# A graph network's attention head: segment scans on scores in PSUM, without the copy to SBUF

## What is computed

```python
h = (x @ W_i).reshape(n, H, C)                      # H = 4 heads, C = 32
e = es[src] + ed[dst]                               # a score for each edge and head
e = where(e > 0, e, 0.2 * e)
m = segment_max(e, dst)
p = exp(e - m[dst])
alpha = p / segment_sum(p, dst)[dst]
out = segment_sum(alpha[:, :, None] * h[src], dst)
```

## Time and profile before

| | us |
|---|---|
| device time, median of 3 (lowest to highest) | 9148.24 (9145.92 to 9149.09) |
| span of the profiled execution, first to last instruction | 9145.7 |
| VectorE busy | 5425.3 (59%) |
| GpSimd busy | 5269.3 (58%) |
| TensorE matmul busy | 5627.4 (62%) |
| ScalarE busy | 4499.0 (49%) |

### The profile page before, as it was taken

The page is one execution under the profiler, slowest core; times in us unless marked ns, Lnnn a source line. Parts: engine busy times, 40 slices in busy tenths (PEclk is TensorE's granted clock), DMA queues, the critical chain, the costliest instruction groups (busy, mean ns, idle before and its releaser), DMA issues.

```text
span 9145.7 us, 130431 instructions
## 1 busy us (share of the span) xinstructions
PE 5627.4 (62%) x34288; PEld 4519.0 (49%) x34288; DVE 5425.3 (59%) x12708; ACT 4499.0 (49%) x8146; POOL 5269.3 (58%) x5192
## 2 busy tenths in 40 slices
PE   4999879974555555555455555555534545445456
PEld 3777646653444454544344545454434444444444
DVE  6888731134666666666466666666645555555555
ACT  2555400014555555554455565555525555555554
POOL 2000100046777777775677777777657777777770
PEclk9999989965555555555555555555555555555558
DMA  3333335504444444443344444444423333333331
GB/s 99 140 139 135 134 131 190 190 8 117 121 118 122 116 125 116 120 119 91 87 121 116 124 116 125 115 121 119 107 64 81 86 81 86 81 86 81 86 81 32
DMA packets 601479, 989.13 MB, mean 108 GB/s; under 512 B 331106, under 2 KB 455043, under 8 KB 561523
## 3 DMA queue, kind: packets, MB, share of 16 engines
q0 software_dynamic: 163760, 357.05, 17.1%
q1 hardware_dynamic: 217540, 544.34, 16.9%
q10 hardware_dynamic: 219648, 81.82, 3.4%
HBM read 758.42 MB, written 224.34 MB: 107 GB/s over the span
## 4 chain that ended last, share of the span: by engine, by line
PE 34%; DVE 18%; DVEq 15%; issue 14%; POOL 13%; DMA 5%; ACT 1%; POOLq 0%; SPq 0%; ACTq 0%
PE bank L979 14%; DVEq L1284 13%; POOL arena L650 12%; PE bank L1202 8%; DVE acc L1882 8%; DMA arena<-row_table,staged_idx 4%; PE bank L1004 3%; PE bank L1130 2%; DVE arena L1838 2%; PE bank L1142 2%; DVEq L1882 1%; DVE arena L1869 1%; DVE x_mem L1556 1%; DVE arena L1831 1%; PE bank L1267 1%
## 5 line engine op out<-in xcount | busy, mean ns | idle before, releaser
L650 POOL DMA_INDIRECT arena<-row_table,staged_idx x4992 | 4982.4, 998 | 1622.7 <-issue 1490.7
L1202 PE MATMUL bank<-arena 128*128 128x136 f32 x9984 | 2504.4, 432 | 1193.0 <-DVE acc L1882 900.5
L1202 PEld LDWEIGHTS bank<-arena 128*128 128x128 f32 x9984 | 2211.2, 318 | 1378.6 <-issue 1372.7
L1882 DVE TENSOR_TENSOR acc<-acc,bank 128x136 f32 x4992 | 1476.6, 296 | 1062.5 <-issue 778.0
L806 ACT ACTIVATE pick_dist<-col,dst_local 128x128 bf16<-128x128 f32 x4992 | 1522.0, 387 | 293.0 <-issue 244.3
L979 PE MATMUL bank<-arena 128*128 128x385 bf16 (+1 forms) x7546 | 1342.6, 327 | 49.5 <-DVE arena L1660 33.0
L598 POOL TENSOR_TENSOR arena<-acc,node_stat 128x896 f32 x14 | 24.4, 1744 | 1730.4 <-POOLq L610 956.4
L1158 PE MATMUL bank<-ident,arena 128*32 128x128 f32 x624 | 161.5, 414 | 1279.5 <-DVE arena L1801 1279.5
L979 PEld LDWEIGHTS bank<-arena 128*128 128x128 bf16 x7546 | 711.7, 98 | 475.9 <-DVE arena L1660 33.2
L1798 DVE TENSOR_TENSOR arena<-arena 128x128 f32<-128x128 f32 x156 | 60.8, 390 | 1320.5 <-DMA arena<-row_table,staged_idx 1320.5
L1869 DVE TENSOR_TENSOR arena<-arena,bank 128x528 f32<-128x528 f32 x1248 | 829.0, 685 | 0.5
(11 more groups left out here) (356 smaller groups left out, 5959.8 us busy)
## 6 DMA issues: line engine op xcount, KB each, us to landing
arena<-dst_rows SPq DMA_DIRECT2D x156, 1024.0 KB, 5.8
cell_rows<-arena SPq DMA_DIRECT2D x76, 1568.0 KB, 5.1
arena<-cell_rows SPq DMA_DIRECT2D x76, 1568.0 KB, 6.5
arena<-row_table,staged_idx POOLq DMA_INDIRECT x4992
edge_stats<-x_mem ACTq DMA_DIRECT2D x416, 192.0 KB
x_mem<-in_edge_attr SPq DMA_DIRECT2D x208, 192.0 KB
x_mem<-segment_flags SPq DMA_DIRECT2D x416, 96.0 KB
arena<-change_rows SPq DMA_DIRECT2D x312, 64.0 KB
```

The source lines that it names most:

```text
L650: pool.indirect_dma_start(gathered[:, at, :], None, table, bass.IndirectOffsetOnAxis(staged_idx[:, at:at + 1], 0)).then_inc(att_gathered[n ...
L1202: mm = pe.matmul(region(k)[:, 0:ROW], pick[:, k, :], gathered[:, b * GROUP + k, :], start=True, stop=True)
L1882: done = dve.tensor_tensor(row, row, region(m * BATCH + k), ALU.add)
```

## The change

The copy of `grp` to SBUF is gone, and so is its tile. The reversed scan of `first_scans` reads `grp` where it read `seg_f`, with no drain before it. In `last_scans` the two corrections are made in `grp` itself in PSUM, the forward scan reads and writes `grp` in place, and the reversed scan reads it from there.

```diff
@@ L218
         seg_m = over(2560, GROUP, 512)
-        grp_sb = over(3072, GROUP, 512)
@@ first_scans
                     dve.tensor_tensor_scan(seg_f, start_flag[:, b, :], grp, FAR, ALU.add, ALU.max)
-                    then()
-                    dve.tensor_tensor_scan(seg_m[:, ::-1], end_flag[:, b, ::-1], seg_f[:, ::-1], FAR,
+                    dve.tensor_tensor_scan(seg_m[:, ::-1], end_flag[:, b, ::-1], grp[:, ::-1], FAR,
                                            ALU.add, ALU.max).then_inc(att.firsts, 1)
@@ last_scans
                     dve.tensor_copy(cross_rows[:, :], bank[0:GROUP, 2, CROSS_AT:CROSS_AT + 2 * HEADS])
-                    dve.tensor_copy(grp_sb, grp)
                     then()
-                    dve.tensor_tensor(grp_sb[:, 0::P], grp_sb[:, 0::P], cross_rows[:, 0:HEADS], ALU.max)
+                    dve.tensor_tensor(grp[:, 0::P], grp[:, 0::P], cross_rows[:, 0:HEADS], ALU.max)
                     then()
-                    dve.tensor_tensor(grp_sb[:, P - 1::P], grp_sb[:, P - 1::P], cross_rows[:, HEADS:2 * HEADS],
-                                      ALU.max)
+                    dve.tensor_tensor(grp[:, P - 1::P], grp[:, P - 1::P], cross_rows[:, HEADS:2 * HEADS], ALU.max)
                     then()
-                    dve.tensor_tensor_scan(seg_f, start_flag[:, b, :], grp_sb, FAR, ALU.add, ALU.max)
+                    dve.tensor_tensor_scan(grp, start_flag[:, b, :], grp, FAR, ALU.add, ALU.max)
                     then()
-                    dve.tensor_tensor_scan(seg_m[:, ::-1], end_flag[:, b, ::-1], seg_f[:, ::-1], FAR,
+                    dve.tensor_tensor_scan(seg_m[:, ::-1], end_flag[:, b, ::-1], grp[:, ::-1], FAR,
                                            ALU.add, ALU.max).then_inc(att.maxima, 1)
```

## The result

The changed kernel takes 8995.2 us in the median of four runs (8993.0 to 9000.7), the kernel before beside it 9147.1 (9143.9 to 9149.1): a ratio of 0.983, 95% interval 0.982 to 0.985. The forecast was 9001 us in 8935 to 9070, faster. One execution of e2 (11928 us) and one of e11 (11367) lie far above the others of the same kernel and are left out of the ratios.

What follows compares the result with a forecast made beforehand. GpSimd's gathers were taken to bound the attention layers, with VectorE's time hidden. Savings of 63.2 (layer three), 82 (layers one and two) and 2.3 us (layer ends) make 147.5, giving 9001 us, range 8935 to 9070.

Steps and rivals of the forecast that it cites:

- The bound: Attention layers: GpSimd's gathers pace them; VectorE waits 8.5 us a group, so its 0.76 us cut is hidden there.
- A two-SBUF-input scan holds the gather that begins in it to its end, a PSUM input frees it: VectorE scans: gathers beginning in two-SBUF-input scans are stretched, 270 us excess in all; one PSUM input stretches nothing.
- Layer three: Third attention layer has only this head's scans, so all its 63.2 us of gather excess goes.
- Layers one and two: First two attention layers: excess falls from 1.99 to 1.2 us a group, 82 us less over 104 groups.
- the first pair: First L1556/L1558 statistics scans of a group, layers one and two: 0.7 us excess taken, between 0 and 1.03.
- the second: Second L1556/L1558 statistics scans of a group, layers one and two: 0.5 us excess taken, 0.99 before.
- PSUM written in place: Corrections and last scans in grp: no added cost taken; bounds 0.15 us more per correction, 2.4 us per scan.
- The layers' ends: Behind each layer's last gather VectorE's shorter work counts: 3 x 0.76 = 2.3 us.
- nothing lifted: Rival: PSUM input does not free the gathers; only 2.3 us go, 9146 us; chance 0.07.
- PSUM slow: Rival: L1838, L1840 and reversed L1810 are slow in PSUM, exceeding 3.6 us of room; 9410 us; chance 0.04.
- the first pair always missed: Rival, layers one and two: first statistics scans catch no gather, second cost 0.2 us; 252 us saved, 8897; chance 0.12.

Runs made afterwards that it cites:

- e2: The changed kernel with the first scans put back as before (reversed scan reads seg_f in SBUF, after a drain); 9089.5 us, ratio 0.994.
- e11: The changed kernel plus first-scan drain, scores copy to SBUF, a second drain and a tiny copy; 10274.2 us beside 10238.9 on a chip with pauses.
- e4: The changed kernel with the first-scan drain and the unread copy of the scores to SBUF put back; 8958.3 us, ratio 0.979.
- e10: The changed kernel with four more scans in last_scans of every group, each with one PSUM input and a drain behind; 9294.3 us in one execution.
- e1: The kernel before with only the first scans changed (reversed scan reads grp in PSUM, no drain); 9027.1 us, ratio 0.987.
- e5: The changed kernel with an extra scan per group in layer three, both inputs in SBUF; 10331.7 us beside 10350.2 on a chip with pauses.
- e6: The changed kernel with an extra scan per group in layer three, one input in PSUM; 10343.0 us beside 10350.2 on a chip with pauses.
- e3: The changed kernel with the drain between the two first scans put back; 8930.9 us, ratio 0.976.
- e9: The changed kernel with first-scan drain, scores copy to SBUF and a second drain behind the copy; 8955.6 us, ratio 0.979.
- e8: The changed kernel with first-scan drain, scores copy and a second drain behind it; 10344.2 us beside 10350.2 on a chip with pauses.

## Why the prediction was right

*The bound.* GpSimd's gathers pace the attention layers and VectorE's time is hidden: right, by the waits after and by e4 (VectorE's old length, 187 us faster). VectorE waits 8 us a group for the gathers, but its room is not that large: in e10 the gathers wait for TensorE's sums, which wait for VectorE, once 2.8 us a group are added.

*A two-SBUF-input scan holds the gather that begins in it to its end, a PSUM input frees it.* Right, and shown by e1 and e2 scan by scan and by the pair e5 and e6. It is wider than the forecast says: the plain `tensor_tensor` L1857 holds gathers too.

*Layer three.* 63.2 us forecast, 63.4 measured.

*Layers one and two.* 1.2 us a group forecast, 1.12 measured: the first pair 0.60 for the 0.7 chosen between 0 and 1.03, the second 0.50 for 0.5. That makes 90.8 us for 82. L1555 moved by 0.13 us against the grid for the 0.16 forecast (11.20 behind the last gather, 11.33 before), the second pair by 0.71 for 0.76. That the first pair would cost more than before in some groups and nothing in others is what came: 25 of 104 are free, 4 were.

*PSUM written in place.* Taken as free: L1834 takes 1.22 us, L1830 and L1832 0.16 each for 0.15. Both bounds, 2.4 and 0.30, were far off.

*The layers' ends.* From a layer's last gather to the next one's first, and to the end, 2.5 us for 2.3. This agreement is luck: the three ends gave 0.05, 1.15 and 1.26 us for 0.76 each, and in e4, with VectorE's old length, the three together are 1.9 us shorter than before the change. The term is too small to be told from the spread.

The sum, 63.4 + 90.8 + 2.5 = 156.7, is 9.9 more than the spans differ. 9.4 of it is the time before the first gather (2099.4 us for 2090.0), where nothing was changed; in e3, e9 and e10 it is 2088, 2091 and 2087. So the profiled execution meets the forecast of 9001 partly by luck: the pairs gave 9 us more than forecast, and the later start took 9 away. The median of the four runs lies 6 us below it.

The rivals: nothing lifted, PSUM slow, and the first pair always missed all failed. The last of these is what e3 then made true for the first pair with a drain, at 8931; its second pair stayed at 0.44 us, not the rival's 0.2. The slower rival's sum was off: it takes off the 82 us that the gathers lose less in layers one and two, which count for nothing once the gathers wait for the sums, and its 3.6 us of room was read at one gather. It put the edge of slower at 5.0 us a group added; e10 adds 5.4 less the 0.76 that the change took away, 4.6, and is already 148 us slower than before.

**A version that beats both** is e3: the changed kernel with the drain in the first scans, 0.976 of before, for 0.983. It is fragile, since 0.07 us decide.

## What to carry to other kernels

When GpSimd's gathers are the bound, look at their longest durations and lay VectorE's instructions beside them: what matters is not how long VectorE works but whether an instruction with two SBUF inputs is running when a gather begins. One operand moved to PSUM frees it. Where none can be moved, the instruction's place against the grid of gathers counts: here 64 us, for the 152 of the change. Then a shorter instruction stream can lose time and a longer one gain it, so count such cuts by what they hold, not by their length, and put them back one at a time.

## What was not expected of the hardware

Two of the chips run the kernel before in 10239 and 10350 us. There the gathers stop for 2.9 us on the mean, about 470 times in e8's three layers. All but some 50 of these stops come before the first gather of a quarter, where GpSimd waits for TensorE's sums (L646 before); the others come before the second. The profile's waits of e8:

```profile
POOL arena L650 <- remote: 841.0, 260, 4.3
...
DVE acc L1882 <- remote: 624.0, 114, 14.9
```

"remote" is its word for a releaser that it cannot find. VectorE has such stops too, before L1882 up to 14.9 us, and the pace is no longer the gathers' alone. Whether VectorE's time counts on such a chip stays open: e11, with about 0.25 us a group more of it than the kernel before, is 0.3% slower (156 x 0.25 = 39 us, 35 measured), but e8, with 0.05 us a group more, is 6 us faster than the kernel before and not 8 slower. What stops the engines there, and what the change by itself brings there, was not tried.

The edges of the hold are sharp. Over all scans of the kernel after, no gather that begins up to 0.096 us after the start of L1555 is held and all from 0.100 are; for L1557, which follows another scan directly, the edge lies at 0.06 to 0.07; and a held gather ends 0.75 to 0.78 us after the scan that holds it. With places read from an old trace the times came out to 0.1% for the change and for e3 and e4; e1 and e9 missed by 0.5 and 0.7%, where places came out other than forecast.
